# A wait for the landed rows of the group ahead, in front of each group of eight gathers on GpSimd

## The reference

```python
ft = (feat @ W).reshape(n, H, OUT)                 # H = 4 heads, OUT = 64; feat = layernorm(x)
e_src = jnp.sum(ft * w_att_src, axis=-1, keepdims=True)
e_dst = jnp.sum(ft * w_att_dst, axis=-1, keepdims=True)
e = e_src[src] + e_dst[dst]
e = jnp.where(e >= 0, e, NEG_SLOPE * e)
ex = jnp.exp(e - segment_max(e, dst)[dst])
a = ex / segment_sum(ex, dst)[dst] * dist
x = x + segment_sum(ft[src] * a, dst).reshape(n, H * OUT)
x = x + moe(layernorm(x))                          # router, softmax, top 2 of 6, three-layer experts
```

## Time and profile before

| | us |
|---|---|
| median of 3 runs | 4007.06 |
| lowest, highest | 4005.75, 4013.24 |
| the profiled execution | 4011.02 |
| its span, first to last instruction | 4009.3 |

### The profile page before, as it was taken

How to read it: one execution, slowest core, us unless ns; L and a number is a source line. 1 busy time by engine, 2 the same in 40 slices (tenths; PEclk the granted TensorE clock), 3 DMA queues, 4 the chain that set the end, 5 groups by cost and what they waited for, 6 DMA issues and landing times. The chain is left out here.

```text
span 4009.3 us, 53462 instructions
## 1 busy us (share of the span) xinstructions
PE 2354.5 (59%) x10832; PEld 1861.4 (46%) x10833; DVE 1938.4 (48%) x4409; ACT 1508.2 (38%) x2731; POOL 2092.1 (52%) x2068
## 2 busy tenths in 40 slices
PE   5733444445544445545455555555556489999995
PEld 4522333333433334434333444444444368777774
DVE  5443344445444445545555565556566683333332
ACT  5612222223332333323333443344444345444443
POOL 0045655555555554554454454444544167777776
PEclk9956667677776777777776776776777789999998
DMA  5433433343433333433333333333433324445453
GB/s 153 161 85 99 107 99 105 102 112 106 110 105 100 110 100 96 112 101 98 100 103 99 96 108 101 101 104 107 113 93 110 92 20 76 79 79 81 80 81 53
DMA packets 231558, 394.55 MB, mean 98 GB/s; under 512 B 55832, under 2 KB 148796, under 8 KB 230881
## 3 DMA queue, kind: packets, MB, share of 16 engines
q0 software_dynamic: 114816, 265.53, 28.2%
q1 hardware_dynamic: 76728, 89.16, 8.3%
q10 hardware_dynamic: 39924, 38.86, 3.0%
HBM read 325.36 MB, written 69.42 MB: 98 GB/s over the span
## 5 line engine op out<-in xcount | busy, mean ns | idle before, releaser
L1001 POOL DMA_INDIRECT m_rows<-table,src_col x1568 | 1498.1, 955 | 1425.8 <-SPq L989 936.6
L1387 PE MATMUL m_A<-m_msg,m_by_edge 128*128 128x260 f32 x3920 | 1313.3, 501 | 1040.4 <-issue 699.8
L1387 PEld LDWEIGHTS m_A<-m_msg,m_by_edge 128*128 128x128 f32 x3920 | 972.6, 256 | 1295.5 <-issue 1096.6
L1085 DVE TENSOR_TENSOR m_msg<-m_rows,m_A 128x2048 f32<-128x2048 f32 (+1 forms) x294 | 568.2, 1933 | 144.3 <-issue 126.1
L1053 DVE TENSOR_REDUCE m_e_sum<-m_E 128x64 f32<-128x192 f32 x295 | 104.8, 355 | 840.7 <-remote 631.8
L1253 ACT ACTIVATE m_z<-m_z 128x32 f32<-128x32 f32 x295 | 67.4, 229 | 1099.8 <-DVE m_z L1064 807.9
L1245 ACT ACTIVATE m_apart<-m_drow,nid 128x1024 bf16 x297 | 340.9, 1148 | 304.5 <-issue 206.2
L1593 POOL DMA_INDIRECT out<-x_con,x_to_i x206 | 329.0, 1597 | 109.2 <-issue 64.9
L1248 ACT ACTIVATE m_by_node<-m_apart,m_one 128x1024 bf16<-128x1024 bf16 x297 | 341.0, 1148 | 11.6 <-issue 1.7
L1046 DVE TENSOR_TENSOR m_by_edge<-m_A,row 128x1024 f32<-128x1024 f32 (+1 forms) x295 | 307.3, 1042 | 60.7 <-issue 57.2
L1760 DVE TENSOR_TENSOR x_con<-x_X,x_b 128x512 f32<-128x512 f32 x103 | 71.3, 692 | 366.4 <-DMA out<-x_con,x_to_i 329.4
(11 more groups left out here) (249 smaller groups left out, 2414.6 us busy)
## 6 DMA issues: line engine op xcount, KB each, us to landing
m_drow<-dst_row SPq DMA_DIRECT2D x196, 256.0 KB
m_rows<-table,src_col POOLq DMA_INDIRECT x1568
table<-f_rowbuf SPq DMA_DIRECT2D x14, 924.0 KB, 5.1
ydram<-m_y ACTq DMA_DIRECT2D x49, 264.0 KB
m_xb<-in_x ACTq DMA_DIRECT2D x48, 256.0 KB
out<-m_x ACTq DMA_DIRECT2D x48, 256.0 KB
f_xin<-in_x SPq DMA_DIRECT2D x13, 896.0 KB, 6.8
x_w<-in_L_ffn_expert_w SPq DMA_DIRECT2D x18, 256.0 KB, 6.0
```

The costliest lines, as they stand in the source:

```text
L1001: nc.gpsimd.indirect_dma_start(rows[:, g % RING, j, :], None, table, bass.IndirectOffsetOnAxis(ap=K.src_col[:, g, j:j + 1], axis=0)).then_ ...
L1085: v.tensor_tensor(msg[i][:, tiles, 0:D].rearrange("p j (h n) -> p j h n", h=HEADS), rws[:, tiles, 0:D].rearrange("p j (h n) -> p j h n", h ...
L1387: m = t.matmul(psA[i][:, 0:ROW], by_edge[i][:, j, :], msg[i][:, j, :], start=(j == tiles[0]), stop=(j == tiles[-1]))
```

## The change

In front of every group but the first, GpSimd now waits until all eight gathers of the group ahead of it have landed. The wait that is taken out was for the earlier gathers into the same slot. Nothing else is changed.

```diff
             for g in range(NG):
                 if g >= RING:
                     pool.wait_ge(slot_free, g - RING + 1)
-                if g >= RING:
-                    pool.wait_ge(gathered[g % RING], 16 * GT * (g // RING))
+                if g:
+                    pool.wait_ge(gathered[(g - 1) % RING], 16 * GT * ((g - 1) // RING + 1))
                 gather(g)
             for i in range(RING):
                 pool.wait_ge(gathered[i], 16 * GT * NCH)
```

## The result

The changed kernel took 3688.84 us (median of 4, 3680.23 to 3692.31), the kernel before 4006.4 us beside it: a ratio of 0.920, 95% interval 0.918 to 0.922. The later runs add something that the forecast didn't foresee at all: the stalls that the change relieves are a condition of the chip which comes and goes. Where it was absent, the kernel before took 3166 us and the changed one 3567, 12.6% slower.

What follows compares the result with a forecast made beforehand. The prediction took the consumers (DVE, ACT, PE), delayed by long rows of gathers, as the bound. 168 us of relief less 15 and about 3 us for GpSimd's floor gave net -150 us: 3857 us, range 3710 to 4080.

Steps and rivals of the forecast that it cites:

- the first 5 us of a burst look normal: Edge loop, two trace windows: consumers progress 5.2 us in a single group and 6.3 us in a pair before stalling.
- none over about 7 us: Sign of being right: DVE's and ACT's unexplained "remote" waits become fewer, and none lasts over about 7 us.
- with PE's result ready: Argument against a no-change outcome: DVE sat idle 14.36 us in the pair window although PE's lookup result was ready.
- the rows are early nearly everywhere: Reading of the slot ring: SP waits only 19.0 us for gathered rows, so the pace of DVE, ACT and PE sets the end.
- the term 73 x 2.3 = 168 us: Gain in the edge loop: 73 group starts right behind the group ahead, each costing 2.3 us net, would be relieved.
- GpSimd's floor: GpSimd's least time per group of eight gathers: claimed to rise from 10.05 to about 11.8 us, below the present periods.
- an equation with three coefficients for four stretches: Fit of edge-loop periods: a constant of 11.12 to 11.50 us, 5.3 us per half item, 2.3 us per back-to-back start.
- The check by two windows: Compared progress in one traced pair of groups with two single groups; gave 1.6 us per back-to-back start.
- The bounds for the gap: Extra time before each of 73 back-to-back group starts on GpSimd: 1.3 to 2.1 us, taken as 1.5 us.
- the last stretch: Sign of being right: gain mostly before 2386 us, the final 45 periods of the edge loop within 20 us of 740.
- Rival A: Delay without relief: a short pause never clears the pile-up, 73 x 1.5 us reaches the path, 4117 us; chance 0.20.
- Rival C: Larger gain: first 100 groups at 12.0 us, other 95 at 14.0; set at 3640 to 3740 us; chance 0.10.

## Why the prediction was right or wrong

**Right: the sign, and most of the mechanism.** GpSimd's bursts stall the others, a burst does so only from some 5 us on ("the first 5 us of a burst look normal"), and a gap in which the rows land clears it. The "remote" waits fell to 6.7 us at the longest ("none over about 7 us"), and no gap between groups is under 2.08 us ("no gap under 1.3"). The readings under it were partly off. DVE's 14.36 us of idle time in the earlier trace rows are not all "with PE's result ready": PE ended at 780.76 us and DVE began at 791.42, 10.7 us late. The first 5 us count for a group with a gap in front, not for one that starts back to back. And "the rows are early nearly everywhere" rested on the 19.0 us of the earlier trace rows, where SP stood 336 us.

**Wrong: the term 73 x 2.3 = 168 us.** This is the step that failed: what a back-to-back start costs. The runs show 331 us in place of 168, that is 4.5 us a start, and they don't show one price: by stretch 22/28, 87/20, 149/19 and 73/6 give 0.8, 4.4, 7.8 and 12 us. The first is small because GpSimd's floor cuts it off. The last can't be a price of six starts alone, for single groups were relieved too: in the kernel before the 66 bursts of one group held 3.0 slow register instructions of DVE each, in the changed kernel a group holds 1.7.

The term came from an equation with three coefficients for four stretches, in which the back-to-back starts fall from 0.56 to 0.13 while half items rise from 0.10 to 0.87. A constant that fits within 0.2 us proves nothing there. Its other two coefficients are off as well. Where neither the stalls nor GpSimd set the pace, in the quiet kernel with half the gathers, the periods of 5.98, 8.00, 9.75 and 11.68 us make about 7.4 us a half item over 5.2 us. Where GpSimd does, in the quiet kernel before, 31 half items in place of 5 change nothing: 509/50 = 10.2 us against 504/50 = 10.1. So a quiet period isn't a sum of these parts but the larger of two: GpSimd's 10.1 us and the consumers' 5.2 + 7.4 h give 10.1, 10.1, 10.1 and 11.6 us, measured 10.1, 10.1, 10.2 and 11.6 (522/45, from start to start). What the stalls add to it in the kernel before is 143, 209, 274 and 208 us in the four stretches, and the fit had spread that over all three of its coefficients; which got how much isn't shown. The check by two windows (1.6 us) failed too: the pair of the earlier trace rows was a mild one, its stall over 0.9 us behind the last gather. In the pair at 2400 us the stall ended 3.5 us behind it.

**Wrong: the floor.** Forecast 11.8 us a group, measured 12.4 (the median period) to 12.5. The gap is 2.6 us, not 2.0. The landing was right: forecast 1.8 us behind the last gather, measured 1.84. The step from there to the next gather wasn't: no run shows the 0.25 to 0.3 us that the forecast took for GpSimd's waking, nor 0.25 us for each step of SP (0.06 us, from 264.93 to 264.99 us in front of the earlier trace rows); the next gather starts 0.77 us behind the landing. The bounds for the gap (1.3 to 2.1 us beyond the 0.3) ended below the 2.3 that was paid. The figure of the Trainium skill, page "DMA: Bandwidth & Descriptors", section "Anatomy of one DMA — SWDGE (gpsimd) path", 2.0 us, is nearer to the landing than to the gap that a kernel sees; the row of 2.62 us decides. With the new floor the wait isn't hidden, as the forecast had it, but is the bound in the first three stretches.

**Wrong: the last stretch.** "Within 20 us of its 740": it took 667.

**Rival A.** Its row, a pause of 2.59 us behind a pair, was real, though the next stall began 3.1 us into the burst (374.62 - 8.92 - 362.59) and not 2.7. A pile of two groups isn't the pile that the change leaves. Its point of decision was sound. Its arithmetic, that each delay reaches the path, is what happens on a quiet chip, by another mechanism: GpSimd is the bound there and 166 gaps grow by 2.3 us.

**Rival C** named the outcome: the first 100 groups at 12.0 us (measured 12.5) and the other 95 at 14.0 (13.6). Its chance of 0.10 was too low. The trace held a reason for more: the unexplained idle times ran to 17 us while the forecast gave back 2.3 us for each pair. But its reason, a stall that starts some 3 us later than in a single group, isn't what the traces show. Between 5 and 6.25 us into a group 33 of 877 register instructions were slow, against 43 of 506 behind the long gaps of the kernel before: rarer, not 3 us later. In part, then, it had the number by luck. Its upper end doesn't follow either: half of C's gain gives 3835 us, halfway from 3857 to 3663 is 3760, and neither is 3740.

**Missed:** that the stall could be a condition of the chip. Nothing in one trace could show that. It could have been asked, for the prediction itself said that no mechanism was visible.

## What to carry to other kernels

A wait that the profile can't put down to anything in the program may not belong to the program: run the kernel on another chip or at another time before a change is built on it. Here the same change is worth -8% in one condition and +12.6% in the other, and a kernel before that takes 4006 us where it can take 3166 is itself the finding. When several coefficients are drawn from few stretches, look for one row or run that moves one of them alone, such as the same group with and without the event, or a kernel in which another engine sets the pace. And where a trace has lost events, its lists of who waited for whom are short by them: the times of the waiting engine's own instructions are not.

## What the runs showed of the hardware

In the stalled condition a row of gathers on GpSimd at a pitch of 1.26 us slows the sequencers of other engines from some 5 us on. Single register instructions then take about 0.7 us (1.4 us at most) where the median on DVE, ACT and SP is some 0.05 us: in the kernel before 621 of 7010 on DVE, 249 of 3654 on ACT and 116 of 817 on SP, but only 22 of 3298 on PE. DVE's instructions came 2 to 6 us apart, and one result of PE was taken 10.7 us late, with GpSimd's gathers (953 ns) and their pitch unchanged. With a gap of 2.5 us between bursts of eight the condition costs 123 to 136 us instead of some 840, with one of 1.2 us about 680. In the quiet condition the same rows show no such wait. The trace also keeps few of the gathers' landing events when stalled, 3575 for the kernel before against 24,952 quiet, so records are lost or merged on the same occasions. The cause wasn't found.

The granted clock moved with it: 0.77 over the span of the kernel before when stalled, 0.85 when quiet, on the same instructions, and PE's matmuls took 2354.5 us there and 2213.4 us here.
